# A two-layer decoder on one core: the mixture's down projection in split float16, the weight slices and the first ternary matrix elsewhere in the queues

## The reference

```python
x = x + attn0(norm(x))        # 16 heads of 16, rotary, causal
x = x + xattn0(norm(x), ctx)  # norm rounded to fp8 in blocks of 128, times the rounded context
x = x + mixture(norm(x))      # 16 experts of 176, 4 chosen, and 2 shared ones
x = x + attn1(norm(x))        # ternary weights, int8 activations
x = x + hashed(norm(x))       # 4 experts of 256, chosen by token id
x = x + ffn1(norm(x))         # ternary weights, inner width 1024
```

## Time and profile before

| | us |
|---|---|
| median of 3 runs (lowest, highest) | 683.1 (682.59, 686.07) |
| the profiled execution | 683.42 |
| its span | 681.6 |
| TensorE busy (share of the span) | 586.2 (86%) |
| VectorE busy | 416.4 (61%) |
| ScalarE busy | 298.4 (44%) |
| GpSimd busy | 124.7 (18%) |

### The profile page before, as it was taken

One profiled execution on the slowest core, in us unless ns is written; L12 is line 12 of the kernel. 1 busy time (PEld: TensorE's weight loads), 2 busy tenths in 40 slices (PEclk: granted clock), 3 DMA queues, 4 the chain that ended last, 5 costly groups with the idle time before them and its releaser, 6 DMA issues.

```text
span 681.6 us, 11559 instructions
## 1 busy us (share of the span) xinstructions
PE 586.2 (86%) x4703; PEld 399.8 (59%) x4746; DVE 416.4 (61%) x993; ACT 298.4 (44%) x470; POOL 124.7 (18%) x162
## 2 busy tenths in 40 slices
PE   2588768889999889998899999999999987888776
PEld 1334434446776567776667777677767645546444
DVE  3568896883557655368525664337545673566585
ACT  2325236337541167512566225771349537532443
POOL 2246054230000410000140000400004010120442
PEclk9799999999999899999979999999999999998969
DMA  6036022110000100000001000010020000000000
GB/s 214 0 123 264 1 98 58 41 62 1 1 2 1 62 1 1 2 1 1 0 15 50 1 2 1 1 62 1 1 93 2 1 1 0 1 1 16 0 16 31
DMA packets 5408, 21.03 MB, mean 31 GB/s; under 512 B 843, under 2 KB 3019, under 8 KB 4460
## 3 DMA queue, kind: packets, MB, share of 16 engines
q1 hardware_dynamic: 5356, 20.30, 8.5%
HBM read 19.25 MB, written 1.05 MB: 30 GB/s over the span
## 4 chain that ended last, share of the span: by engine, by line
PE 58%; DVE 27%; ACT 8%; issue 5%; DMA 1%; POOL 0%; SPq 0%; ACTq 0%; DVEq 0%
PE ps L883 18%; PE ps L914 16%; DVE nmx L1657 4%; PE ps L657 4%; ACT L1354 2%; PE ps L771 2%; PE ps L893 2%; PE ps L679 1%; DVE y L1554 1%; PE ps L712 1%; PE ps L752 1%; PE ps L744 1%; PE ps L707 1%; PE ps L641 1%; ACT hs L1354 1%
## 5 line engine op out<-in xcount | busy, mean ns | idle before, releaser
L1766 DVE TENSOR_TENSOR hs<-hs,ps 128x512 f32<-128x512 f32 (+1 forms) x68 | 45.5, 669 | 103.7 <-PE ps L883 57.9
L914 PE MATMUL ps<-w2f,hs 128*128 128x256 f32 x400 | 101.0, 397 | 0.0
L1354 ACT ACTIVATE hs<-ps 128x512 f32<-128x512 f32 (+1 forms) x68 | 39.7, 584 | 119.9 <-PE ps L883 119.6
L914 PEld LDWEIGHTS ps<-w2f,hs 128*128 128x128 f32 x400 | 73.1, 192 | 18.4 <-issue 9.6
L641 PE MATMUL ps<-selh,idb 128*128 128x512 bf16 x314 | 74.4, 379 | 2.5 <-issue 1.1
L504 POOL TENSOR_TENSOR ve<-mv,half 128x2 f32<-128x2 f32 x24 | 4.7, 196 | 381.9 <-DVE mv L1547 381.9
L1657 DVE TENSOR_REDUCE nmx<-ps 128x2 f32<-128x512 f32 (+1 forms) x96 | 61.0, 680 | 6.1 <-PE ps L712 5.7
L641 PEld LDWEIGHTS ps<-selh,idb 128*128 128x128 bf16 x334 | 31.2, 98 | 35.8 <-issue 2.1
L1313 ACT ACTIVATE pk<-ps 128x512 f32<-128x512 f32 x64 | 34.7, 595 | 18.3 <-PE ps L755 18.1
L1354 ACT ACT_TABLE_LOAD x33 | 42.3, 1283 | 0.6
L883 PE MATMUL ps<-yah,w3h 128*128 128x256 f16 x200 | 39.1, 278 | 3.7 <-DVE hs L1772 3.7
(11 more groups left out here) (234 smaller groups left out, 1184.2 us busy)
## 6 DMA issues: line engine op xcount, KB each, us to landing
stage<-in_w SPq DMA_DIRECT2D x8, 800.0 KB, 4.2
tstage<-in_tern SPq DMA_DIRECT2D x4, 1024.0 KB, 4.8
w2f<-in_w SPq DMA_DIRECT2D x1, 3200.0 KB, 14.2
cs<-in_ctxT SPq DMA_DIRECT2D x1, 1024.0 KB, 10.2
cd<-in_ctxT SPq DMA_DIRECT2D x1, 1024.0 KB, 4.6
out_x<-xs SPq DMA_DIRECT2D x4, 256.0 KB, 2.2
w0s<-in_w SPq DMA_DIRECT2D x1, 768.0 KB, 6.8
xs<-in_x SPq DMA_DIRECT2D x1, 768.0 KB, 8.1
```

Of the source, the lines that this page charges most:

```text
L914: mm = pe.matmul(ps[:, bank, j * D:(j + 1) * D], hs[:, n % 4, par * S + j * P:par * S + (j + 1) * P], w, start=(first and par == 0 and j = ...
L1354: act.activation(hs[:, n % 4, 0:w], ps[:, gate_bank(n), 0:w], ACT.Silu).then_inc(e_sil.sem, 1)
L1766: TT(hs[:, n % 4, 0:w], hs[:, n % 4, 0:w], ps[:, up_bank(n), 0:w], ALU.mult).then_inc(e_hb.sem, 1)
```

## The change

- The down weights are split like the others, into `w2h` and `w2l` (float16, together the size of `w2f`). The inner values of a pair are split too: `inner_high` on ScalarE copies `hs` to float16 `hh`, `inner_low` on VectorE subtracts to float16 `hl` (two buffers each). `hs` keeps three buffers. `down` issues three float16 products, high by high, high by low and low by high, where it issued one in float32. The hashed experts' down product stays float32.
- `inner_high(k - 1)` stands directly before the Silu of pair k, `inner_low(k - 1)` directly before `times_up` of pair k; in the cross attention's part, that of pair 7 stands between the fourth maximum and the context's norm.
- The last pair's split, its `down`, `experts_added` and the moments behind it go to the beginning of the next phase. There `down` follows the first scores.
- The slices are 12, in a ring of three places of `stage`: two of W1 and W3, four of W2, six of W1 and W3. ScalarE handles slices 0 to 8 in phase 0 and 9 to 11 in phase 1. GpSimd does low halves 0 to 5 ahead of the context's norm of phase 0; before slice 6 it waits until the maxima of phase 1 are turned (`m_ok`), and does slices 7 to 11 behind the router's norm. TensorE waits for 12 low halves before phase 2.
- `magnitudes(0)` stands behind the third exponential of phase 2, `ternary(0)` before the context's norm of phase 2.

The diff, without the semaphores' declarations:

```diff
+def is_mixture(it):
+    return 2 <= it < 2 + B
+W_SLICES = 3 * B
+STAGES = 3
...
-        w2f = sb("w2f", [P, W_COLS], F32)
+        w2h = sb("w2h", [P, W_COLS], F16)
+        w2l = sb("w2l", [P, W_COLS], F16)
-        stage = sb("stage", [P, 3, W_SLICE], F32)
+        stage = sb("stage", [P, STAGES, W_SLICE], F32)
-        hs = sb("hs", [P, 4, 512], F32, at=stage_at)
+        hs = sb("hs", [P, 3, 512], F32, at=stage_at)
+        hh = sb("hh", [P, 2, 512], F16, at=stage_at + 6144)
+        hl = sb("hl", [P, 2, 512], F16)
...
+        def slice_of(q):
+            n, part = (2, q - 2) if 2 <= q < 2 + B else (q % 2, q // 2 if q < 2 else q // 2 - B // 2)
+            cols = slice(part * W_SLICE, (part + 1) * W_SLICE)
+            high, low = (wh[n], wl[n]) if n < 2 else (w2h, w2l)
+            return (w1, w3, w2)[n][:, cols], high[:, cols], low[:, cols]
...
 # SP
-            for b in range(B):
-                if b == 1:
-                    sp.dma_start(w2f[:, :], w2).then_inc(d_w2.sem, 16)
-                for n, w in enumerate((w1, w3)):
-                    if b:
-                        sp.wait_ge(wst_lo.sem, wst_lo.at(b - 1, n + 1))
-                    sp.dma_start(stage[:, n, :], w[:, b * W_SLICE:(b + 1) * W_SLICE]).then_inc(d_wst[n].sem, 16)
-            sp.wait_ge(wst_lo.sem, 2 * B)
+            for q in range(W_SLICES):
+                if q >= STAGES:
+                    sp.wait_ge(wst_lo.sem, q - STAGES + 1)
+                sp.dma_start(stage[:, q % STAGES, :], slice_of(q)[0]).then_inc(d_wst[q % STAGES].sem, 16)
+            sp.wait_ge(wst_lo.sem, W_SLICES)
...
 # GpSimd
             rsqrt_ln("head", 1)
-            for n in range(2):
-                split_lo(0, n)
+            for q in range(6):
+                split_lo(q)
             rsqrt_ln("context", 0)
             rsqrt_ln("head", 2)
-            split_lo(1, 0)
-            split_lo(1, 1)
+            g.wait_ge(m_ok.sem, 2)
+            split_lo(6)
             rsqrt_ln("router", 0)
-            for n in range(2):
-                split_lo(2, n)
-            split_lo(3, 0)
+            for q in range(7, W_SLICES):
+                split_lo(q)
             rsqrt_ln("context", 1)
             rsqrt_ln("head", 3)
-            split_lo(3, 1)
             rsqrt_ln("router", 1)
+            ternary(0)
             rsqrt_ln("context", 2)
-            ternary(0)
...
 # TensorE, down
-                    pe.wait_ge(e_hc.sem, n + 1)
+                    pe.wait_ge(e_lo.sem, n + 1)
+                    terms = [(hh[:, n % 2], w2h), (hh[:, n % 2], w2l), (hl[:, n % 2], w2h)]
...
+                    terms = [(hs[:, n % 3], None)]
...
                     for j in range(JT):
+                        for m, (inner, w) in enumerate(terms):
+                            w = cd[:, p, par, :] if w is None else w[:, (2 * p + par) * D:(2 * p + par + 1) * D]
+                            mm = pe.matmul(ps[:, bank, j * D:(j + 1) * D],
+                                           inner[:, par * S + j * P:par * S + (j + 1) * P], w,
...
-                if 0 < k <= count:
+                if 0 < k <= count and (k < MOE_PAIRS or not is_mixture(it)):
                     down(first + k - 1)
+            def down_left(it):
+                if is_mixture(it):
+                    down(MIXED[it][0] + MOE_PAIRS - 1)
...
                 scores_exp(it, 0)
+                down_left(it - 1)
                 gates(it, 0)
...
 # ScalarE
+            def inner_high(n):
+                act.wait_ge(e_hc.sem, n + 1)
+                if n >= 2:
+                    act.wait_ge(e_dn.sem, n - 1)
+                w = tiles_of(n) * S
+                act.activation(hh[:, n % 2, 0:w], hs[:, n % 3, 0:w], ACT.Copy).then_inc(e_hi.sem, 1)
             def sil(it, k):
+                first, count = MIXED.get(it, (0, 0))
+                if k and is_mixture(it):
+                    inner_high(first + k - 1)
...
 # ScalarE, phase_a
+                high_left(it - 1)
                 exponentials(it, 0)
...
                 exponentials(it, 2)
+                if it == 2:
+                    magnitudes(0)
...
                 exponentials(it, 4)
                 sil(it, 4)
+                if it == 0:
+                    slices(3)
                 stacks(it + 1, 1)
                 exponentials(it, 5)
+                if it == 0:
+                    slices(4)
+                if it == 1:
+                    slices(11)
...
                 turned_queries(it + 1, 1)
-                if it == 1:
-                    slices(3, 0)
-                if it == 2:
-                    magnitudes(0)
+                if it == 0:
+                    slices(5)
...
 # VectorE
+            def inner_low(n):
+                dve.wait_ge(e_hi.sem, n + 1)
+                w = tiles_of(n) * S
+                TT(hl[:, n % 2, 0:w], hs[:, n % 3, 0:w], hh[:, n % 2, 0:w], ALU.subtract).then_inc(e_lo.sem, 1)
             def hb(it, k):
+                first, count = MIXED.get(it, (0, 0))
+                if k and is_mixture(it) and not (k == 8 and it < B):
+                    inner_low(first + k - 1)
...
+            def mixture_ended(it):
+                if is_mixture(it):
+                    inner_low(MIXED[it][0] + MOE_PAIRS - 1)
+                    experts_added(it - 2)
+                    if it < ITS - 2:
+                        moments_of("head", it + 2)
...
 # VectorE, phase_b0
                 own(it, 7)
                 maximum(it + 1, 3)
+                if is_mixture(it):
+                    inner_low(MIXED[it][0] + 7)
                 normalised("context", b)
```

More of the change, by code:

```diff
@@ L343, in decoder @@
         d_sel = sig("d_sel")
-        d_wst = [sig(f"d_w{n}", 16) for n in (1, 3)]
+        d_wst = [sig(f"d_wst{n}", 16) for n in range(STAGES)]
         d_ts = sig("d_ts", 16)
@@ L506, in rsqrt_ln, with split_lo @@
                 g.tensor_tensor(rstd[:, ln % 2, :], ve[:, ln % 2, :], half[:, 0:2], ALU.pow).then_inc(rstd_ok.sem, 1)
-            def split_lo(b, n):
-                g.wait_ge(wst_hi.sem, wst_hi.at(b, n + 1))
+            def split_lo(q):
+                g.wait_ge(wst_hi.sem, q + 1)
+                _, high, low = slice_of(q)
                 for a in range(0, W_SLICE, LOW_PIECE):
-                    cols = slice(b * W_SLICE + a, b * W_SLICE + a + LOW_PIECE)
-                    last = g.tensor_tensor(wl[n][:, cols], stage[:, n, a:a + LOW_PIECE], wh[n][:, cols], ALU.subtract)
+                    cols = slice(a, a + LOW_PIECE)
+                    last = g.tensor_tensor(low[:, cols], stage[:, q % STAGES, cols], high[:, cols], ALU.subtract)
                 last.then_inc(wst_lo.sem, 1)
@@ L910, in down @@
                     bank, first, final = gate_bank(n), True, True
+                    terms = [(hs[:, n % 3], None)]
                 for par in range(last + 1):
-                    w = w2f[:, (2 * p + par) * D:(2 * p + par + 1) * D] if kind == "moe" else cd[:, p, par, :]
                     for j in range(JT):
-                        mm = pe.matmul(ps[:, bank, j * D:(j + 1) * D],
-                                       hs[:, n % 4, par * S + j * P:par * S + (j + 1) * P], w,
-                                       start=(first and par == 0 and j == 0), stop=(final and par == last),
-                                       skip_group_check=True)
+                        for m, (inner, w) in enumerate(terms):
+                            w = cd[:, p, par, :] if w is None else w[:, (2 * p + par) * D:(2 * p + par + 1) * D]
+                            mm = pe.matmul(ps[:, bank, j * D:(j + 1) * D],
+                                           inner[:, par * S + j * P:par * S + (j + 1) * P], w,
+                                           start=(first and par == 0 and j == 0 and m == 0),
+                                           stop=(final and par == last and m + 1 == len(terms)),
+                                           skip_group_check=True)
                 mm.then_inc(e_dn.sem, 1)
@@ L1350, in silu_of, with high_left @@
                 act.wait_ge(e_a.sem, n + 1)
-                if n >= 4:
-                    act.wait_ge(e_dn.sem, n - 3)
+                if n >= 3:
+                    act.wait_ge(e_lo.sem if n - 3 < ALL_MOE else e_dn.sem, n - 2)
                 w = tiles_of(n) * S
-                act.activation(hs[:, n % 4, 0:w], ps[:, gate_bank(n), 0:w], ACT.Silu).then_inc(e_sil.sem, 1)
-            def sil(it, k):
-                if k < MIXED.get(it, (0, 0))[1]:
-                    silu_of(MIXED[it][0] + k)
+                act.activation(hs[:, n % 3, 0:w], ps[:, gate_bank(n), 0:w], ACT.Silu).then_inc(e_sil.sem, 1)
+            def inner_high(n):
[4 more added lines that the diff above has]
+                act.activation(hh[:, n % 2, 0:w], hs[:, n % 3, 0:w], ACT.Copy).then_inc(e_hi.sem, 1)
+            def sil(it, k):
+                first, count = MIXED.get(it, (0, 0))
+                if k and is_mixture(it):
+                    inner_high(first + k - 1)
+                if k < count:
```

(20 more changed lines are left out.)

34 lines of the change are left out of this document (17 added, 17 removed).

## The result

The changed kernel takes 674.93 us (median of 4 runs, 674.74 to 676.79) against 683.38 before: ratio 0.988, 95% interval 0.985 to 0.992. The forecast was 673.5, in a range of 665 to 683. In a second comparison the same kernel took 676.34 (6 runs, ratio 0.990, 0.986 to 0.994). The profiled execution took 676.79, the longest of the four and 6.6 less than the profiled one of before.

What follows compares the result with a forecast made beforehand. TensorE was taken to bound phases 2 to 5, TensorE and VectorE together phase 0. The terms -26.8 - 3.6 + 14.4 + 0.5 + 3.0 + 2.5 = -10.0 took 683.42 us to about 673.5, range 665 to 683.

Steps and rivals of the forecast that it cites:

- The down product: TensorE, phases 2 to 5: float16 takes 1.31 us a pair instead of 1.92; 44 pair-equivalents on the chain give 26.8 us.
- The split work: High copies on ScalarE and low subtractions on VectorE in phases 2 to 5 delay TensorE's inputs, costing 14.4 us together.
- collisions: GpSimd's ternary passes meet VectorE's low-half subtractions three times in the mixed phases, 1.0 us each, 3.0 in all.
- The places in phases 2 and 3: ScalarE's copies delay Silus; VectorE's low halves of pairs 7 and 8 delay norm and up-multiplication, the latter 2.8 us together.
- VectorE's idle: Phases 4 and 5, 378.4 to 404.7 in one: short waits not fully usable for subtractions, 1.5 us lost each, 3.0 together.
- ScalarE's places: Phases 2 to 5: copies between fourth and sixth exponentials cost 4.4 us; before Silus of pairs 5 and 1, 2.4 and 1.8.
- The ternary matrix: Phase 2: moving GpSimd's passes earlier removes late waits, gaining 3.6 us, less 0.5 for ScalarE's magnitudes delaying a Silu.
- Phases 0 and 1: Twelve weight slices instead of eight on ScalarE and GpSimd make these phases 2.5 us slower, from -1 to +7.
- a sign that I am wrong: The forecast would be wrong if the first two phases together changed by more than 7 us.
- the fourth rival: Slice ring and GpSimd's exclusion of two-input VectorE operations drag the first two phases 13.9 us, total 684.8; chance 0.12.
- The last pair: Moved behind the next phase's first scores: only the half pair's gain already counted with the float16 product, nothing more.
- Two readings named ahead: No 3 us idle before TensorE late in phase 2; sixth exponential no earlier than 6.8 us after the fifth.

Runs made afterwards that it cites:

- experiment 12: The kernel before with only the first ternary matrix's magnitudes and GpSimd passes moved earlier in phase 2: 680.60 us, ratio 0.994 to the kernel before.
- experiment 5: The changed kernel with the first ternary matrix's magnitudes and passes back in their old place: 678.20 us, ratio 0.989 to the kernel before.
- experiment 7: The changed kernel with GpSimd subtracting 16 columns instead of 1600 for each of the four down-weight slices: 672.28 us, ratio 0.984 to the kernel before.
- experiment 8: The changed kernel with 31 instead of 7 unused TensorE products ahead of phase 0's first stack turn: 673.93 us, ratio 0.984 to the kernel before.
- experiment 1: The changed kernel with the down product left in float32 and no split of the inner values: 680.20 us, ratio 0.996 to the kernel before.
- experiment 6: The changed kernel with each phase's last pair split, multiplied and added at its own phase's end: 677.27 us, ratio 0.990 to the kernel before.

## Why the prediction came out right, and where it did not

The mechanisms were right: the float16 product saves time on TensorE's path, the split work takes most of it back, the slices cost something in phase 0. That the total came within 1.4 us of the median is luck: terms that were 5.9 and 5.6 us too good and others 3.8 and 2.75 us too bad nearly cancelled, and the profiled execution, taken for itself, misses by 3.4. Term by term, forecast against measured (two profiled executions: -10.0 against -6.6):

- **The down product, -26.8 against -20.9.** The mis-sized term is the piece. I took 1.31 us for twelve float16 matmuls from a gate product; in the chain the down product itself shows 1.42, so 0.50 a pair is saved instead of 0.61. The chain of before had this figure too, for gate products in another place:

```profile
366.59 1.42 PE ps L883 x12
```

```profile
377.99 1.42 PE ps L933 x12
```

  The timelines say the same: from its start to the next product's, one down product takes 1.83 before (first fence) and 1.32 after.

```profile
235.93 1.99 PE L914 MATMUL ps<-w2f,hs 128*128 128x256 f32 x8
237.76 0.38 PE L883 MATMUL ps<-yah,w1h 128*128 128x256 f16 x2
```

```profile
235.53 0.28 PE L933 MATMUL ps<-w2h,hh 128*128 128x256 f16 x1
...
236.85 0.28 PE L743 MATMUL ps<-idb,mtok 128*128 128x128 bf16 x2
```

  44 x 0.50 = 22.0 is near the 20.9, which fits the count of what stood on the path; the runs don't count the pieces one by one. All pieces of a chain run from the end of the record before them to their own end, so what stands ahead of one changes its figure: the gate product of 364.52 and fourteen others directly behind a down product take 1.31, that of 366.59 behind the attention's short products 1.42. A down product stands behind the share product, and 1.92 and 1.42 are both measured there; I had set 1.92 from that place against 1.31 from the other. By the rule of the Trainium skill that I had set beside it (FP8 and Floating Point Precision, TensorE Precision Notes: 4 passes, so 0.44 a pair, 19.2 in all) this term would have been nearer to 20.9 than by my 0.61; the measured 0.50 lies between, and decides.
- **The split work, +14.4 and collisions +3.0, against +13.6.** By phase the forecast had 4.7, 3.7, 4.8 and 4.2, the collisions included; measured 5.0, 3.9, 3.2 and 1.5. The places in phases 2 and 3 were sized well, though one is another: the low half of pair 8 stood behind the router's choice of experts and TensorE waited 2.14 us for the low half itself, not for the up-multiplication. In phases 4 and 5 it cost 4.3 us less than forecast. That VectorE's idle took up the subtractions, which I had denied it, would explain up to 3.0 of that; no run parts it from ScalarE's places and the collisions.
- **The ternary matrix, -3.1 against -3.3 beside the float32 product** (experiment 12), and about 0.6 in the changed kernel, by the one pair of profiles with equal clock (experiment 5). The price was right for the kernel it was read from; it did not carry over to the kernel with the split, where both edits change the same queues.
- **Phases 0 and 1, +2.5 against +8.1,** and above 7, which I had named as a sign that I am wrong. Phase 0 fails: 5.4 of its 5.96 us go with four low halves on GpSimd (experiment 7). I gave the two-input operations 1.0 between 64 and 82 us, where each of five loses 0.6 to 0.7 in a row with TensorE behind, and left out the clock, 2.5 (experiment 8). It is the mechanism of the fourth rival in half its size, but without its ring: with ScalarE's copies left in place phase 0 is 0.55 longer than before, no more. Phase 1's 2.15 are the clock: where it held, the same queue took 50.9, 0.8 shorter than before. Over the nine profiles of that queue the mean is 52.4; the two with the queue of before have 51.66 and 52.44. Whether the longer wait for the first query copy (1.45 us instead of 0.67) makes the fall more frequent is not shown.
- **The clock in phase 4, nothing forecast, -2.75** in experiment 1; the changed kernel's own profile kept a part of it. **The last pair, nothing, against -1 to -2** (experiment 6).

With the measured terms: -20.9 + 13.6 - 3.3 - 2.75 + 8.1 leaves -5.25. The last 1.4 to -6.6 are 0.9 in phases 2 to 5, where the moved pair is the likely cause, and 0.8 from phase 6 on, less 0.3 ahead of phase 0. The page's chain of the changed kernel covers only 45% of the span, so ScalarE's share can't be set against the earlier trace rows. Two readings named ahead held: no idle of 3 us late in phase 2 (1.00 now); 7.0 to 8.2 us from the fifth to the sixth exponential in phases 2 to 5. Two signs failed: phase 0 grew by 5.96, not by 0 to 3, and phase 3, to be shorter by 2 to 6, gained nothing: the product's 4.8 less the split's 3.9 there stand against 0.9 that experiment 1 is longer than before, at a granted clock of 0.98 where that had 1.00; no run parts its cause.

What stays open: the three collisions with the second and third ternary matrices were not tried alone.

## What to carry to other kernels

Price an operation from its start to the next instruction's start, or from pieces of the chain that stand behind the same kind of instruction. When work is moved onto GpSimd, list every VectorE instruction with two SBUF inputs in that stretch that TensorE waits for, charge each up to one piece of the GpSimd operation, and add the clock if TensorE then idles longer than its filler covers. Test a gain of 2 us with fillers in place, or the clock's chance hides it: moving the low half of pair 8 gave nothing in the total without them and was part of 9.5 us with them, though its own share there was not measured.

## What the hardware showed that was not expected

- A 256-column subtraction on VectorE takes 0.42 us alone and 1.05 to 1.16 beside GpSimd's subtractions, a 2048-column one 2.28 and 3.02: the loss, 0.6 to 0.7, is the same for both, below the 0.91 of one of GpSimd's pieces (3.65 / 4). The other way round, the first three pieces of GpSimd's first low half took 2.64, 1.92 and 1.92 us, against 0.94 undisturbed: each began while VectorE worked on 2048 columns and ended about one piece after that instruction (L1602 until 55.17, L1532 until 57.06 and L1534 until 58.94 in the kernel before). L1532 and L1534 have only one input, so two inputs are not needed to hold GpSimd up. The Trainium skill (SBUF — State Buffer, Who interferes with whom) says the two exclude each other for a whole instruction; the trace agrees.
- The same instructions behind the same waits (1.95 us in phase 2; 1.28 and 1.45 in phase 1) ran at the upper clock, 2.4 GHz, in some profiles and at 1.2 in others. Phase 1 took 50.9 us in three profiles of the same queue and 54.5 in two. The kernel before varies from 679.4 to 687.6 over all its runs.
